# Two parts by halves of the tokens in the last routed layer of a four-layer kernel

## The reference

```
x = x + 0.5 * ffn0(layernorm(x))      # moe0: one expert per token, 256 hidden
x = x + attention0(layernorm(x))
x = x + 0.5 * ffn0(layernorm(x))      # moe2
x = x + 0.5 * ffn1(layernorm(x))      # moe3: the best two experts, 512 hidden, biases
x = x + attention1(layernorm(x))
x = x + 0.5 * ffn1(layernorm(x))      # moe6, the last layer
...
probs = softmax(x @ Wr.T); topv, topi = top_k(probs, 2)
y = sum over the two: topv * (gelu(x @ W1[e] + b1[e]) @ W2[e] + b2[e])
```

## Time and profile before

| what | us |
|---|---|
| median of 3 runs (lowest, highest) | 1372.99 (1368.29, 1379.28) |
| the profiled execution | 1385.0 |
| its span, from the first to the last instruction | 1381.8 |
| last layer: until the pair loop is under way (1135 to 1168) | 33 |
| last layer: pair loop (1168 to 1295) | 127 |
| last layer: results brought home, end (1295 to 1382) | 87 |

### The profile page before, as it was taken

The page is one execution under the profiler, slowest core; times in us unless marked ns, Lnnn a source line. Parts: engine busy times, 40 slices in busy tenths (PEclk is TensorE's granted clock), DMA queues, the critical chain, the costliest instruction groups (busy, mean ns, idle before and its releaser), DMA issues.

```text
span 1381.8 us, 20947 instructions
## 1 busy us (share of the span) xinstructions
PE 702.9 (51%) x6007; PEld 570.3 (41%) x6015; DVE 788.8 (57%) x2469; ACT 488.0 (35%) x1079; POOL 539.4 (39%) x539
## 2 busy tenths in 40 slices
PE   3313660357735224821445999235767435999300
PEld 3312440136635113511434889213445423888300
DVE  7574463667784762644562556438878671556322
ACT  4300330344434001311303778325455202878200
POOL 3006627034430016255425662460431106663376
PEclk9999995578865555965556999768788655999755
DMA  9201311000001002311101333110110001234222
GB/s 290 77 0 36 70 51 53 3 1 0 0 18 46 0 12 56 65 54 57 31 15 51 77 78 59 52 42 3 37 32 16 23 4 51 75 78 69 56 76 75
DMA packets 82018, 65.29 MB, mean 47 GB/s; under 512 B 10634, under 2 KB 73610, under 8 KB 81954
## 3 DMA queue, kind: packets, MB, share of 16 engines
q1 hardware_dynamic: 68226, 36.49, 9.2%
q0 software_dynamic: 13728, 28.02, 8.7%
HBM read 38.52 MB, written 25.95 MB: 47 GB/s over the span
## 4 chain that ended last, share of the span: by engine, by line
PE 32%; DVE 30%; issue 13%; POOL 11%; another core or an unknown queue 7%; ACT 4%; DMA 3%; DVEq 0%; POOLq 0%; ACTq 0%
POOL rt L1014 9%; PE bank L599 4%; PE bank L620 4%; PE bank L601 3%; PE bank L600 3%; PE bank L621 3%; PE bank L623 3%; DVE rt L779 3%; PE bank L390 2%; DVE nwt L298 1%; DVE stats L351 1%; PE bank L583 1%; DVE nwt L299 1%; PE bank L528 1%
## 5 line engine op out<-in xcount | busy, mean ns | idle before, releaser
L994 POOL DMA_INDIRECT turned<-xrows_moe,token x234 | 242.5, 1036 | 374.3 <-DVE token L865 246.6
L1014 POOL DMA_INDIRECT rt<-y_moe,slot_i x192 | 183.8, 957 | 155.7 <-DMA y_moe<-arena 91.7
L682 ACT ACTIVATE turned<-bank,b1T 128x256 f32<-128x256 f32 x312 | 122.2, 474 | 161.1 <-PE bank L601 117.5
L599 PE MATMUL bank<-rt,w1h 128*128 128x256 bf16 (+1 forms) x468 | 128.1, 274 | 45.7 <-issue 20.6
L620 PE MATMUL bank<-w2h,turned 128*128 x780 | 142.4, 225 | 12.2 <-issue 10.7
L621 PE MATMUL bank<-w2h,turned 128*128 x780 | 142.2, 225 | 8.6 <-issue 8.2
L887 DVE TENSOR_TENSOR turned<-turned 128x1024 bf16<-128x1024 f32 (+1 forms) x118 | 122.5, 1038 | 38.5 <-ACT turned L686 27.9
L623 PE MATMUL bank<-w2l,turned 128*128 x780 | 123.8, 225 | 7.8 <-issue 7.8
L600 PE MATMUL bank<-rt,w1h 128*128 128x256 bf16 (+1 forms) x468 | 127.4, 272 | 0.0
L601 PE MATMUL bank<-rt,w1l 128*128 128x256 bf16 (+1 forms) x468 | 127.1, 272 | 0.0
L933 DVE SCALAR_TENSOR_TENSOR x<-rt,small,x 128x128 f32<-128x128 f32 x192 | 62.2, 352 | 109.1 <-DMA rt<-y_moe,slot_i 98.8
(11 more groups left out here) (280 smaller groups left out, 1793.7 us busy)
## 6 DMA issues: line engine op xcount, KB each, us to landing
y_moe<-arena SPq DMA_DIRECT2D x118, 128.0 KB
xrows_moe<-xn SPq DMA_DIRECT2D x8, 512.0 KB, 3.8
turned<-xrows_moe,token POOLq DMA_INDIRECT x234
rt<-y_moe,slot_i POOLq DMA_INDIRECT x192
x<-in_x SPq DMA_DIRECT2D x4, 512.0 KB, 5.7
arena<-in_w SPq DMA_DIRECT2D x1, 2048.0 KB, 9.6
xn<-in_w SPq DMA_DIRECT2D x8, 256.0 KB, 4.4
xrows_moe<-arena SPq DMA_DIRECT2D x4, 512.0 KB, 3.2
```

Of the source, the lines that this page charges most:

```text
L599: nc.tensor.matmul(o, wh, xh_t, start=True, stop=False)
L682: last = nc.scalar.activation(s["h32"][:, k % 2, o], bank[1 + 2 * (k % 2) + u // 2][:, W * (u % 2):W * (u % 2) + W], ACT.Gelu, bias=b1T[:, ...
L994: nc.gpsimd.indirect_dma_start(out=s["xs"][:, 2 * (t % BODY) + j], out_offset=None, in_=s["xdram"], in_offset=bass.IndirectOffsetOnAxis(ap ...
L1014: nc.gpsimd.indirect_dma_start(out=ytok[:, at % TOK], out_offset=None, in_=s["ydram"], in_offset=bass.IndirectOffsetOnAxis(ap=slot_i[:, k, ...
```

## The change

moe6 gets `parts=2`. Slots are sorted by half of the tokens first and by expert within a half, so the first half's slots all lie in the first 39 tiles. ALIGN becomes 128 for it, so each expert and half is padded to 128, the count of pairs stays 39, and each pair holds two units, each with its own expert (PER = 2). So `up` and `down` of PE take the form that K = 1 has, with FC = 4 and biases; ACT has eight activations of 128 columns; the copy to bf16 is split, one half on ACT, the other on DVE. The experts of the units are worked out after the token list. POOL, from pair 32 on, brings home 4, 4, 4, 3, 2, 1, 1 tiles of the first half's results ahead of the gathers of pairs 32 to 38, and the other 45 at the end. The ring for them is 32 tiles, in arena, and DVE waits for four at a time. The core of the diff:

```diff
@@ moe @@
+            s["align"] = P if parts == 2 else ALIGN[K]
+            s["per"] = W // s["align"]
+            s["hop"] = NT // parts
@@ moe_tensor @@
-            PER = 3 - K
+            PER = s["per"]
...
-                    for j, (at, width) in zip(js, ((0, P), (P, P))) if K == 1 else ((0, (0, W)),):
+                    for j, (at, width) in zip(js, ((0, P), (P, P))) if PER == 2 else ((0, (0, W)),):
...
-                        nc.tensor.matmul(y[j], selector[:, ds(e[0][1], P)], b2rows, start=(j == 0), stop=False)
+                        nc.tensor.matmul(y[j], selector[:, ds(e[j % PER][1], P)], b2rows, start=(j == 0), stop=False)
...
-                    for group in [(j,) for j in js] if K == 1 else (js,):
+                    for group in [(j,) for j in js] if PER == 2 else (js,):
@@ moe_scalar @@
+            def biased(t, k, es):
                 waits(t)
+                wide = W // len(es)
                 for u in range(FC):
+                    for j, e in enumerate(es):
+                        o = slice(W * u + wide * j, W * u + wide * (j + 1))
+                        i = slice(W * (u % 2) + wide * j, W * (u % 2) + wide * (j + 1))
+                        last = nc.scalar.activation(s["h32"][:, k % 2, o], bank[1 + 2 * (k % 2) + u // 2][:, i],
+                                                    ACT.Gelu, bias=b1T[:, ds(e + u, 1)])
                 last.then_inc(s["gelu"], 1)
                 act.wait_ge(*s.at("gelu", t + 1))
-                nc.scalar.activation(s["hh"][:, k % 4], s["h32"][:, k % 2], ACT.Copy).then_inc(s["act"], 1)
+                o = slice(0, FC * W // s["parts"])
+                nc.scalar.activation(s["hh"][:, k % 4, o], s["h32"][:, k % 2, o], ACT.Copy).then_inc(s["act"], 1)
@@ moe_vector @@
+            if parts == 1:
+                unit_experts()
             dve.wait_ge(*s.at("inv", 2 * K))
             nc.vector.tensor_scalar(token[:, 0:tiles], bank[7][:, 0:tiles], T / 2, None, ALU.add).then_inc(s["idx"], 1)
+            if parts == 2:
+                unit_experts()
...
             def low(t, k):
                 r = k % 2
+                if s["parts"] == 2:
+                    o = slice(FC * W // 2, FC * W)
+                    dve.wait_ge(*s.at("gelu", t + 1))
+                    dve.wait_ge(*s.at("down", t + 1))
+                    nc.vector.tensor_copy(s["hh"][:, k % 4, o], s["h32"][:, r, o]).then_inc(s["high"], 1)
+                    dve.wait_ge(*s.at("high", t + 1))
                 dve.wait_ge(*s.at("act", t + 1 + RING))
@@ combine @@
-                    dve.wait_ge(brought[at % TOK], BROUGHT[s["index"]] + 16 * (at // TOK + 1))
+                    if s["parts"] == 2:
+                        y = ytok2[:, at % TOK2]
+                        dve.wait_ge(brought[K * quad + k], BROUGHT[s["index"]] + 16 * QUAD)
...
@@ moe_pool @@
+        EARLY_AT = 32
+        EARLY = (4, 4, 4, 3, 2, 1, 1)
...
             for t in range(s["pairs"]):
                 if t >= BODY:
                     pool.wait_ge(*s.at("turned", t - BODY + 1))
+                if s["parts"] == 2 and t == EARLY_AT:
+                    for r in range(YRING):
+                        pool.wait_ge(ystored[r], YSTORED[r][s["index"]] + 16 * len(range(r, -(-s["pairs"] // 2), YRING)))
+                if s["parts"] == 2 and t >= EARLY_AT:
+                    for i in range(EARLY[t - EARLY_AT]):
+                        bring_one(pool, s, first_part)
+                        first_part += 1
@@ moe_bring_all @@
+            if s["parts"] == 2:
+                for at in range(sum(EARLY), s["K"] * NT):
+                    bring_one(pool, s, at)
+                return
```

More of the change, by code:

```diff
@@ L39 @@
 C_RESET = 520
-C_ROW = C_RESET + 256
+C_ROW = C_RESET + 512
 C_END = C_ROW + 1
@@ L489, in moe @@
                                        xhi=(2 - K) * (n // 2), onehot=2 * K,
-                                       inv=2 * K, idx=1, half=(K - 1) * NT, turned=n // 2, up=n // 2, gelu=n // 2 * bias, comb=NT,
+                                       inv=2 * K, idx=1, half=(K - 1) * NT, turned=n // 2, up=n // 2, gelu=n // 2 * bias, high=(parts - 1) * (n // 2), comb=NT,
                                        **{q: RINGS[q] + n // 2 for q in RINGS}))
@@ L645, in moe_tensor @@
                     down(t, k, e[k])
-            packs = [packed(PER * loops)]
+            packs = [packed(PER * loops + i) for i in range(-(-PER * rest // BODY))]
             e = [expert(packs, k) for k in range(rest)]
@@ L745, in prefix_sums @@
                                            bank[6][:, 256:512].rearrange("p (t e) -> p e t", e=E)))
-                done(nc.vector.tensor_tensor_scan(rt[:, R_INC, :], reset, tot, 0.0, ALU.mult, ALU.add))
+                done(nc.vector.tensor_tensor_scan(rt[:, R_INC, :], resets[:, s["parts"] - 1], tot, 0.0, ALU.mult, ALU.add))
                 done(nc.vector.tensor_tensor(rt[:, R_A, :], rt[:, R_INC, :], tot, ALU.subtract))
@@ L852, in moe_vector @@
                 nc.vector.memset(srch[:, 23:24], 0.0).then_inc(s["onehot"], 1)
-            pairs = s["pairs"]
-            done(nc.vector.tensor_tensor(tcmp, starts[:, 2 if K == 1 else 0].unsqueeze(2).to_broadcast([1, UNITS, E]),
-                                         end[0:1].unsqueeze(1).to_broadcast([1, UNITS, E]), ALU.is_ge))
-            done(nc.vector.tensor_reduce(tsum[:, 0], tcmp, AX, ALU.add))
-            done(nc.vector.tensor_scalar(tsum[:, 1], tsum[:, 0], float(E - 1), None, ALU.min))
@@ L980, in moe_rows_pool, with bring_one @@
                     .then_inc(s["hl"], 1)
+        EARLY_AT = 32
+        EARLY = (4, 4, 4, 3, 2, 1, 1)
+        def bring_one(pool, s, at):
+            group, i = divmod(at, QUAD)
+            quad, k = divmod(group, s["K"])
+            t = s["order"][QUAD * quad + i]
+            if at >= TOK2:
+                pool.wait_ge(*s.at("comb" if k == s["K"] - 1 else "half", QUAD * (quad - TOK2 // (QUAD * s["K"])) + i + 1))
+            nc.gpsimd.indirect_dma_start(
+                out=ytok2[:, at % TOK2], out_offset=None,
+                in_=s["ydram"][0:P * (T // P + E - 1)] if quad < NT // QUAD // 2 else s["ydram"],
+                in_offset=bass.IndirectOffsetOnAxis(ap=slot_i[:, k, t:t + 1], axis=0))\
+                .then_inc(brought[group], 16)
         def moe_pool(pool, s, meanwhile=None):
@@ L1825 @@
     centre = a['L1_attn_w_rel'].shape[0] // 2
+    u = np.arange(2 * (NT + E))
     arrays = {
```

85 lines of the change are left out of this document (53 added, 32 removed).

## The result

The changed kernel takes 1437.8 us as the median of 4 runs (1430.3 to 1440.3); the kernel before took 1373.7 us beside it (4 runs, 1368.3 to 1379.3). The ratio is 1.0457, 95% interval 1.0400 to 1.0514: slower by 4.6%. The profiled execution took 1440.3 us (span 1438.2), where the one before took 1385.0 (1381.8). The forecast was 1407.5 with 1368 to 1440 as range, or +34.5 us, and +64.1 was measured: the side is right, the size 30 us short, and the time lies 2 us inside the range's end.

What follows compares the result with a forecast made beforehand. PE was taken to bound the last layer's loop and POOL its tail. Terms -23.7 + 1.0 + 55.7 + 0.5 + 1.0 gave +34.5 us on the 1373.0 us median: 1407.5 us, range 1368 to 1440.

Steps and rivals of the forecast that it cites:

- Term 1: Last layer's tail: 19 of 64 result gathers move under the loop at 1.248 us each, -23.7 us.
- term 2: Tail: DVE waits for four landed tiles at once, leaving four adds after the last landing, +1.0 us (0 to 1.2).
- at most some 2 us: Loop, pairs 32 to 38: PE's wait behind early gathers, from 41 us of POOL work against 42 us of cycles.
- Term 3: PE in the last loop: address work per weight group makes a pair 4.80 us, was 3.21; +55.7 us (38 to 73).
- waits and loop ends: Last loop: time a pair takes on top of PE's summed phases of 4.56 us, taken as 0.24 us.
- lower bound of 4.3: PE's cycle in the loop, in us: all small parts at their low ends and half of the waits gone.
- the stall of 18 us: Before the last layer's loop runs: ACT's 17.97 us stall doesn't grow with the longer body, 0 (-2 to +5).
- The start: Before the last loop runs: stall change 0 (-2 to +5), later table of experts per unit +0.5 us (0 to 1.5).
- the last pairs: End of the loop: the last two down-projections have 0.5 us more each, half behind ACT, +1.0 us (0 to 2).
- the unit table: Last layer's start: table of experts per unit made after the token list, +0.5 us (0 to 1.5).
- A clock below 1 in the loop: Sign of being wrong; its rival: PE with holes gets the lower clock, cycle 6.3 us, 1460 us, chance 0.06.
- The rule weighed: PE's 128-column matmuls sustain about 81 ns, so a new pair's 54 matmuls take 4.37 us before waits.

Runs made afterwards that it cites:

- fixed addresses: Changed kernel with PE's weight and bias addresses in the last layer constant, experts 0 and 1 for every pair: 1230.8 us, ratio 0.9899.
- POOL two ahead: Kernel before, with POOL gathering at most two pairs ahead of PE's transposes instead of eight, in all four routed layers: ratios 1.0072, 1.0091, and 0.9591 (1327.5 us).
- the version with one expert to a pair: Changed kernel with each expert's slots of a half padded to 256, 46 pairs, 32 gathers early: 1243.9 us, ratio 1.0013.
- paced: Changed kernel, same 19 early gathers, one ahead of each of pairs 32 to 38, then two after each of six later transposes: ratios 1.0402, 1.0449, 1.0304.

## Why the prediction was right, and where it was short

- **Term 1, the tail (-23.7).** Right: -22.4 with term 2 in it (-22.7 by the forecast), and 24.6 us with against without early gathers. Its clause that PE would wait "at most some 2 us" even at 3.2 us a cycle was wrong: with a PE that fast, fixed addresses cost it 14 us. The 42 us of thirteen cycles were set against 41 us of gathers as one sum; but POOL's work for pair 32 alone is 4 + 2 gathers, 7.5 us, and so on for three pairs, and each pair's rows are due in its own cycle. It did no harm here, as PE was slow.
- **Term 3, PE's cycle (+55.7, 38 to 73).** The mechanism is confirmed by taking it away: same matmuls, fixed addresses, 3.0 us. The undisturbed pair came to the hundredth, 4.81 measured, but that is luck, since it stands against the wrong sum: I had 4.56 before waits. Up 2.16 for 2.22, down 1.98 for 1.84, transposes 0.42 for 0.30, bias 0.25 for 0.20: the last two at their high ends, and the down-projection above a value for which I had no range. And "waits and loop ends" were 0.4 us, not 0.24: the mean pair has 5.18 to 5.22. The lower bound of 4.3 was no sum of its parts either; at their low ends and with half of the waits they give 4.5. The seven cycles of the earlier trace rows that gave 0.23 do not contain an end of the loop body; the eight cycles of one body average 5.19 us here (5.5, 6.0, 5.2, 5.1, 5.5, 4.8, 4.8, 4.6), and in the body, besides the pairs, stand the loop's close and three loads of the experts' numbers (`packed`), which no run took out one by one. The loop without the slow stretches grew by 84.0 - 19 = 65 us, inside the 38 to 73, nine over the value taken. (Counted as the forecast did, from the sixth transposes on, it is 85.7 - 19 = 67: the cycle before them still holds 7 us of stall in the kernel before.)
- **What was missing: the slow stretches, +19 us.** The earlier trace rows had it in view. I read the stall of 18 us as something of a loop's first pass and priced it at 0 (-2 to +5); I didn't ask what POOL did meanwhile. It ran gathers without a pause, as the early ones make it do again. The start itself came to +4.7, at the top of its range. Over the forecast these are 9.3 us of cycle, 19 of slow stretches and 4.2 of start; the last pairs gave 1.2 back, the tail took 0.3: 31.6 us, the distance from +34.5 to the +66.1 of the layer. That the time still lies inside the range, by 2 us, is in part luck: the range was drawn without these 19 us. On the 1241 kind the change costs 54 us.
- **The rest.** ACT, eight activations and a copy in 2.8 us, and DVE stayed under PE; the group waits and the unit table show no cost that can be told apart. The clock was 0.98 and 0.91 in the undisturbed stretches, and 0.76 where PE's instructions came 0.7 us apart. A clock below 1 in the loop was among my signs of being wrong, but it cost nothing that shows: the last five cycles, at 0.94 here, are the same as on the 1241 kind at 1.00 (5.47, 6.29, 5.02, 5.03, 4.70 us on both).
- **The rule weighed,** from the Trainium skill, TensorE: Matmul & The Clock Gate, section Back-to-back issue gap: 81 ns a matmul sustained at 128 columns. The runs show 56 ns in a stream with fixed addresses (fifty matmuls and four transposes in 3.02 us) and 96 ns with computed ones (5.2 us). So 81 is no property of the width in this kernel; it depends on what the stream does between matmuls. The Trainium skill calls 56 ns, in the same section, the gap of an isolated matmul; here a whole stream kept it.

No version that follows the expert choice was seen to beat the kernel before on both kinds of chip. POOL two ahead is the best on the 1374 kind (0.959) and 0.7 to 0.9% slower on the other; a depth between two and eight was not tried, and the version with one expert to a pair was not run on the 1374 kind.

## What to carry to other kernels

Count an engine's instruction stream as a rate of its own beside its array: add up matmuls, address steps, waits and loop ends over one whole loop body (not over a stretch that leaves the closing out), and halve the work behind one address only where the array still has more to do than the stream. Before work is moved under a loop, add up what the engine that takes it has to do from its first to its last instruction: here 142 gathers of 1.25 us set a floor, and a split that adds 14 of them gives its gain back. And when a stall has no releaser, look at what the other engines do in just that time, and try what spreading out unbroken runs of gathers does.

## What the runs showed of the hardware

- On two chips of four, the other engines, PE and ACT above all, were slow to issue while POOL ran indirect gathers without a pause: PE's instructions 0.70 us apart at 66 GB/s of DMA, in runs of 9 to 22 gathers and first in one of six; with runs of up to three gathers (paced) or six (two ahead, once the loop runs) it did not show, so how long a run must be is not settled. On the other two chips it never did, in a run of 156 either. The same kernel takes 1374 to 1377 us on the ones and 1241 to 1242 on the others, 11% apart, so a change is to be judged on both: by their ratios the paced kernel is 1.5% better than the changed one on the first kind, and equal on the second.
- PE's stream runs ahead of the array: up groups with computed addresses ran at 0.17 us where the phase before had left the stream time, and at 0.25 where it had not.
- A pair of address steps (high and low weights of one group) costs the stream some 0.14 us, an estimate from the 5.2 and 4.07 us of a pair with 16 and with 8 groups whose addresses are computed. The 3.07 us with none lie at the array's pace and leave out other steps too.
